# Scores and mask on 64-row tiles, roots seeded by the exponential, norm's scale on ACT, new orders on all engines

## The reference, cut to what matters

```python
qkv = x @ Wqkv                        # 3 x 1024
q, k, v = heads of 64 channels, 16 heads
q = l2norm(q) * qs ;  k = l2norm(k) * ksc
q = q * cos * scale + rotate_half(q) * sin * scale
k = k * cos * inv   + rotate_half(k) * sin * inv
# windows of 32 queries, each sees its own and the former window's 64 keys
sim = einsum('bhwie,bhwje->bhwij', bq, bk2) * 8.0
sim = where(mask, -max, sim)
out = einsum('bhwij,bhwje->bhwie', softmax(sim, -1), bv2)
x = x + out @ Wo
xn = (x - mu) / sqrt(var + 1e-5) * g + bln
a, gate = split(xn @ W1 + b1)
x = x + a * gelu(gate) @ W2 + b2
```

## Time and profile before

| | before |
|---|---|
| median of three runs | 1,781.34 us (1,781.17 to 1,782.97) |
| profiled execution, its own time | 1,780.26 us |
| span of that execution in the profile | 1,778.4 us |
| mean granted TensorE clock, share of full | 0.986 |
| PE, DVE busy | 1,708.9, 1,512.6 us |
| ACT, POOL busy | 1,350.4, 1,355.7 us |
| DMA queue of SP | 261 MB, 57.8% of 16 engines' span |

### The profile page before, as it was taken

How to read it: one execution, slowest core, us unless ns; L and a number is a source line. 1 busy time by engine, 2 the same in 40 slices (tenths; PEclk the granted TensorE clock), 3 DMA queues, 4 the chain that set the end, 5 groups by cost and what they waited for, 6 DMA issues and landing times.

```text
span 1778.4 us, 53112 instructions
## 1 busy us (share of the span) xinstructions
PE 1708.9 (96%) x20416; PEld 1355.0 (76%) x20416; DVE 1512.6 (85%) x2297; ACT 1350.4 (76%) x2689; POOL 1355.7 (76%) x2035
## 2 busy tenths in 40 slices
PE   7999968999999999999999999999999999999986
PEld 5666646888888888788888788887888888888864
DVE  5666648999999999999999999999899999999973
ACT  6777846787777777787777788787777887777763
POOL 6767658878788787778878787878878787887850
PEclk9999989999999999999999999999999999999996
DMA  3567706465865646765566656558464666656462
GB/s 115 184 234 262 254 10 159 107 148 120 223 141 132 145 107 139 213 143 139 123 147 191 152 123 146 124 127 236 112 161 104 149 177 168 147 117 146 109 152 63
DMA packets 101340, 264.54 MB, mean 149 GB/s; under 512 B 26720, under 2 KB 34912, under 8 KB 101088
## 3 DMA queue, kind: packets, MB, share of 16 engines
q1 hardware_dynamic: 101088, 261.13, 57.8%
HBM read 45.02 MB, written 27.26 MB: 41 GB/s over the span
## 4 chain that ended last, share of the span: by engine, by line
PE 81%; issue 2%; DVE 1%; ACT 1%; POOL 1%; POOLq 0%; ACTq 0%; DVEq 0%
PE ps L1462 12%; PE ps L1497 10%; PE ps L1479 10%; PE ps L1464 10%; PE ps L1463 10%; PE ps L1518 9%; PE ps L1568 7%; PE ps L1507 5%; PE ps L1579 3%; PE ps L1492 2%; PE ps L1537 1%; PE ps L1545 1%; DVE rot L1136 1%; PE ps L1554 1%; PE ps L1529 1%
## 5 line engine op out<-in xcount | busy, mean ns | idle before, releaser
L1136 DVE TENSOR_TENSOR rot<-ps,rope_l 128x1024 f32<-128x1024 f32 x384 | 461.8, 1213 | 100.9 <-ACT sq L1283 84.8
L1031 POOL TENSOR_TENSOR rot<-rot 128x512 f32<-128x512 f32 x384 | 485.8, 1288 | 31.5 <-DVE rot L1136 31.5
L1293 ACT ACTIVATE un<-ps 128x512 f32<-128x512 f32 x384 | 224.6, 598 | 237.9 <-PE ps L1464 229.8
L1462 PE MATMUL ps<-w_t,xs_hi 128*128 128x512 f32 x768 | 374.9, 488 | 12.5 <-DVE rot L1136 7.6
L1072 POOL TENSOR_TENSOR rot<-rot,rnorm 128x1024 f32<-128x1024 f32 x192 | 365.5, 1904 | 21.3
L1464 PE MATMUL ps<-w_t,xs_lo 128*128 128x512 f32 x768 | 304.7, 397 | 0.0
L1463 PE MATMUL ps<-w_t,xs_hi 128*128 128x512 f32 x768 | 303.6, 395 | 0.0
L1283 ACT ACTIVATE sq<-ps 128x512 f32<-128x512 f32 x384 | 229.1, 597 | 34.6 <-PE ps L1464 20.1
L1311 ACT ACTIVATE kT<-ps 64x512 f32<-64x512 f32 x384 | 226.3, 589 | 23.7 <-PE ps L1479 20.3
L1479 PE MATMUL ps<-ident_s,rot 128*128 128x128 f32 x1536 | 234.8, 275 | 8.6 <-ACT kT L1311 3.4
L1112 DVE TENSOR_REDUCE ssum<-sq 128x16 f32<-128x1024 f32 x192 | 232.5, 1211 | 9.8 <-ACT sq L1283 9.8
(11 more groups left out here) (121 smaller groups left out, 3093.2 us busy)
## 6 DMA issues: line engine op xcount, KB each, us to landing
vk<-un SPq DMA_DIRECT2D x1440, 128.0 KB, 2.3
w_t<-weights_dram SPq DMA_DIRECT2D x48, 512.0 KB, 6.9
weights_dram<-u_split SPq DMA_DIRECT2D x12, 1024.0 KB, 5.1
weights_dram<-qk_split SPq DMA_DIRECT2D x24, 512.0 KB, 4.0
raw<-wqk_dram SPq DMA_DIRECT2D x24, 256.0 KB, 4.9
wvt_s<-wvt_dram SPq DMA_DIRECT2D x12, 256.0 KB, 4.3
wo_s<-wo_dram SPq DMA_DIRECT2D x12, 256.0 KB, 4.7
w_s<-w_dram SPq DMA_DIRECT2D x6, 341.0 KB, 3.8
```

What stands on the lines that cost most here:

```text
L1031: last = G.tensor_tensor(cos[:, :, s, :], cos[:, :, s, :], sin[:, :, 1 - s, :], ALU.add)
L1136: V.tensor_tensor(dst, src[:, None, :, :].broadcast_to([P, 2, H // 2, D]), tab[:, :, None, :].broadcast_to([P, 2, H // 2, D]), ALU.mult).t ...
L1462: M.matmul(bank, x_hi, w_t[:, j, 0, :], start=True, stop=False)
```

## The change

- **kT** loses its zeros and its second copy: [128, pairs, keys] with the first head of a pair in rows 0 to 63 and the second in rows 64 to 127. ACT copies all 128 rows at once (four copies a unit in place of eight). The memset clears only the 32 columns ahead of the first window.
- **Scores**: each matmul contracts 64 rows of one head with 64 columns; 64 of them a tile in place of 32. The head of a pair picks the row half of the array and the PSUM bank, the window picks 32 columns. The mask is eight matmuls of 64 rows by 32 columns, each with 512 moving columns, in place of two of 64 by 128. The heads stand in the banks in another order, and DVE's scale of the probabilities writes them back in the old one.
- **The root**: the sums are clamped by POOL; the first guess is ACT's exponential of the sum's bits read as an integer; POOL does two Newton steps of four operations (one of them now a TENSOR_SCALAR).
- **The norm's** scale and shift go from DVE to ACT (`feed_scale`).
- **All five orders** are new, with the banks of the projections (`PJ_BANK`, `PJ_BEFORE`) and the order in which SP renews the weights; W2 is loaded ahead of the last value copies of a layer.

The core of the diff:

```diff
-        kT = sb("kT", [P, 2, PAIRS, WIN + T])
+        kT = sb("kT", [P, PAIRS, WIN + T])
...
-                    G.memset(kT[:, 0, :, :], 0.0)
-                    G.memset(kT[:, 1, :, :], 0.0)
+                    G.memset(kT[:, :, 0:WIN], 0.0)
...
+                    pool.wait_ge(ss_d.sem, ss_d.at(n, 2 * t + 1))
+                    G.tensor_scalar(ssum[:, t, :], ssum[:, t, :], 1e-24, None, ALU.max).then_inc(cl_g.sem, 1)
...
-                    pool.wait_ge(seed_d.sem, seed_d.at(n, t))
+                    pool.wait_ge(seed_a.sem, seed_a.at(n, t))
                     y, s = rnorm[:, t, :], ssum[:, t, :]
-                    for i in range(3):
-                        at = 12 * t + 4 * i
+                    for i, c in enumerate(ROOT_STEPS):
+                        at = 8 * t + 4 * i
...
-                        G.tensor_tensor(newton[:, :], thrice[:, i, :], newton[:, :], ALU.subtract).then_inc(newton_g.sem, 1)
+                        G.tensor_scalar(newton[:, :], newton[:, :], -0.5 * c, 1.5 * c, ALU.mult, ALU.add).then_inc(newton_g.sem, 1)
...
-                    V.tensor_scalar(ssum[:, t, :], ssum[:, t, :], 1e-24, None, ALU.max).then_inc(cl_d.sem, 1)
-                    dve.wait_ge(cl_d.sem, cl_d.at(n, t))
-                    V.tensor_scalar(rnorm[:, t, :].bitcast(I32), ssum[:, t, :].bitcast(I32), -0.5, RSQRT_SEED,
-                                    ALU.mult, ALU.add).then_inc(seed_d.sem, 1)
...
-                    V.tensor_tensor(prob[:, t, :].rearrange("p (h k) -> p h k", h=H), tile_scores(t),
-                                    linv[:, t, :, None].broadcast_to([P, H, 2 * WIN]), ALU.mult).then_inc(pn_d.sem, 1)
+                    pairs = prob[:, t, :].rearrange("p (a hp k) -> p hp a k", hp=2, a=PAIRS)
+                    inv = linv[:, t, :].rearrange("p (hp a) -> p hp a", hp=2)[:, :, :, None].broadcast_to([P, 2, PAIRS, 2 * WIN])
+                    V.tensor_tensor(pairs, tile_scores(t).rearrange("p (hp a) k -> p hp a k", hp=2), inv, ALU.mult).then_inc(pn_d.sem, 1)
...
-                    V.tensor_scalar(xg[:, :], xg[:, :], cur[:, u[1] % 2, 0:1], cur[:, u[1] % 2, 1:2], ALU.mult, ALU.add).then_inc(xh_d.sem, 1)
...
-                        for hp in range(2):
-                            rows = slice(64 * hp, 64 * hp + 64)
-                            last = S.activation(kT[rows, hp, pairs, WIN + t * P:WIN + (t + 1) * P], src[rows], ACT.Copy)
+                        last = S.activation(kT[:, pairs, WIN + t * P:WIN + (t + 1) * P], src, ACT.Copy)
...
+                    act.wait_ge(cl_g.sem, cl_g.at(n, t))
+                    S.activation(rnorm[:, t, :], ssum[:, t, :].bitcast(I32), ACT.Exp, bias=root_shift[:, 0:1], scale=ROOT_SLOPE).then_inc(seed_a.sem, 1)
...
+                    S.activation(xg[:, :], xg[:, :], ACT.Identity, scale=col[:, 0:1], bias=col[:, 1:2]).then_inc(xh_a.sem, 1)
...
-                    for hp in range(2):
-                        rows = slice(64 * hp, 64 * hp + 64)
-                        M.matmul(ps[:, SO[t] + hp, :], wpick[rows, t, :], wmask[rows, :, :].rearrange("p a k -> p (a k)"), start=True, stop=False)
+                    for k in range(4):
+                        for hp in range(2):
+                            rows = slice(64 * hp, 64 * hp + 64)
+                            M.matmul(ps[32 * k:32 * k + 32, SO[t] + hp, :], wpick[rows, t, 32 * k:32 * k + 32], wmask[rows, :, :].rearrange("p a k -> p (a k)"),
+                                     start=True, stop=False)
                     for a in range(PAIRS):
                         for k in range(4):
                             w = 4 * t + k
-                            out_s = ps[32 * k:32 * k + 32, SO[t] + a // 4, (a % 4) * P:(a % 4 + 1) * P]
-                            last = M.matmul(out_s, qT[:, par, a, 32 * w:32 * w + 32], kT[:, :, a, 32 * w:32 * w + 64],
-                                            start=False, stop=a % 4 == 3)
+                            for hp in range(2):
+                                rows = slice(64 * hp, 64 * hp + 64)
+                                out_s = ps[32 * k:32 * k + 32, SO[t] + hp, a * 2 * WIN:(a + 1) * 2 * WIN]
+                                last = M.matmul(out_s, qT[rows, par, a, 32 * w:32 * w + 32], kT[rows, a, 32 * w:32 * w + 64],
+                                                start=False, stop=a == PAIRS - 1)
```

More of the change, by code:

```diff
@@ L18 @@
+import math
 from contextlib import ExitStack
@@ L1075, in step @@
                     after, u, last = ((m, s + k) for k in (1, 0, -2))
[L1076 to L1079 removed]
                     feed_rstd(last)
+                    turn(u, 1, 0)
+                    clamp(u, 1)
                     shift_lo(after)
[L1082 removed]
                     norms(u, 1)
@@ L1087, in step @@
                     turn(after, 0, 0)
+                    clamp(after, 0)
+                    norms(after, 0)
+                    normalise(after, 0, 0)
+                    turn(after, 0, 1)
+                    normalise(after, 0, 1)
                 pipeline(pool, step)
@@ L1226, in step @@
                 def step(m, s):
-                    after, u, before, last = ((m, s + k) for k in (1, 0, -1, -2))
+                    after, u, before, last, oldest = ((m, s + k) for k in (1, 0, -1, -2, -3))
+                    rope(u, 0, 1, 0)
+                    rope(u, 0, 1, 1)
+                    soft_sum(before, 0)
+                    feed_4(oldest)
+                    soft_top(before, 1)
+                    feed_1(last)
+                    soft_shift(before, 1)
+                    feed_2(last)
+                    soft_scale(before, 0)
+                    rope(u, 1, 0, 0)
+                    feed_3(last)
+                    rope(u, 1, 0, 1)
+                    sums(u, 1, 0)
+                    feed_norm(last)
+                    sums(u, 1, 1)
+                    rope(u, 1, 1, 0)
                     rope(u, 1, 1, 1)
-                    soft_scale(before, 1)
+                    soft_sum(before, 1)
                     feed_hidden(last, 0)
                     soft_top(u, 0)
+                    soft_scale(before, 1)
                     soft_shift(u, 0)
```

156 lines of the change are left out of this document (70 added, 86 removed).

## The result

| | before | after |
|---|---|---|
| median of four runs | 1,781.69 us | 1,753.76 us (1,745.96 to 1,755.60) |
| ratio to before, 95% interval | | 0.984 (0.981 to 0.986) |
| span of the profiled execution | 1,778.4 us | 1,752.2 us |
| median and mean of the 45 full units | 30.89, 30.95 us | 29.81, 30.39 us |

The kernel became faster by 28 us, where 78 were forecast. A unit's length is read from the starts of POOL's product that writes `rtok`, which comes once a unit. The last row says already that there are two parts to explain: the typical unit became 1.1 us shorter, not 1.7, and some units are much longer than the typical one, which was hardly so before.

A forecast was written before the change was run, and what follows sets the result against it. PE was taken to bound the loop: 2.1 us a unit saved, 1.7 kept after DVE's waits, times 46 units is 78 us, so 1,780.3 becomes 1,702 and the median 1,703. Range 1,680 to 1,730, chance 0.57; 1,680 to 1,790, 0.79.

The forecast's parts named there:

- The bound: Long loop: PE sets the pace at 30.87 us a unit, with DVE's own work at 29.1 us.
- The array as the old stage's limit: Old scores stage: streaming columns, not issue, makes each group of four matmuls take 0.11 us.
- two row groups beside each other: New scores: 64-row matmuls on both row groups run at once, each further pair costing 0.11 us, not 0.22.
- the load not the limit: New scores: small matmuls aren't held by load latency; four loads of 128 columns follow by 0.11 us, here 32.
- rival (b): Scores rounds don't shrink because the load made their 0.11 us; PE saves 0.1 us a unit, 1,772 to 1,790; chance 0.08.
- Sixteen rounds at 56 ns, 0.90 us: New scores stage: each round of 8 records takes about 56 ns, so 16 rounds take 0.90 us.
- rival (c): Scores stage of 136 pairs held by PE's instruction supply; slower, 1,854 us at 22 ns a pair, 1,947 at 29.5; chance 0.16.
- The 25 ns of the page "TensorE: Matmul & The Clock Gate" of the Trainium skill: Matmul starts never under about 25 ns apart: 136 starts 3.4 us a tile, kernel some 110 us slower; not adopted.
- The mask: Mask ahead of the scores: eight matmuls beside each other take 0.27 us, where two took 0.32.
- The stage: Mask and scores together: 1.17 us in place of 2.21, saving 1.04 a tile, 2.1 us a unit.
- The 0.4 us a unit for the new orders: Unit taken as 29.2 us, not PE's 28.8, since the orders are new and DVE has waits.
- rival (a): New orders lose the gain through late ropes or copies holding PE; unit 29.8 to 30.8 us, 1,730 to 1,777; chance 0.14.

The follow-up runs named there:

- half: The changed kernel with head pairs 4 to 7 left out of the scores stage, so 64 of its 128 pairs of instructions are gone; 1,663.5 us.
- newscores: The kernel before with only the new scores, mask, key layout, key copies and softmax scale; 1,767.1 us, 0.993 of before.
- cols32: The changed kernel with each scores product taking 32 of its 64 key columns, same number of instructions; 1,750.2 us.
- padded: The whole changed kernel with 243 one-column matmuls added in nine places ahead of values stages; 1,745.9 us, 0.982 of before.
- paced: The changed kernel with the old two-matmul mask and 181 one-column matmuls added in the projections of four units; 1,745.2 us, 0.978 of before.

## Why the prediction was wrong, point by point

- **The bound.** Right. PE bounds the loop before and after, and half shows that it would go on to do so down to 28.3 us.
- **The array as the old stage's limit; two row groups beside each other; the load not the limit.** Right: sixteen records go in two rounds of 56 ns, and rival (b) falls.
- **Sixteen rounds at 56 ns, 0.90 us.** This is the step that failed. It took the pace of a burst's first pairs for that of 128 pairs. Two rounds go at 56 ns, the third at 75, the rest at 67 to 123, and the products take 1.35 us. The text named the doubt itself, in rival (c): the first pairs "may have been queued while PE drained". The pace fits that. The bound was set at 29.5 ns a pair, the rival priced at 22, and the truth, 1.35 us for 128, is 10.5 ns. With the mask it is 1.72 us for 136, 12.6 ns: under break-even at 16.3, so the sign held and the gain shrank. It would have been better to give values between 7 and 16 ns a chance of their own.
- **The 25 ns of the page "TensorE: Matmul & The Clock Gate" of the Trainium skill** (section "Wait — 56ns, not 53.3ns?"). They gave an estimated 3.4 us a tile; 1.72 was measured. Over eight tiles the rule doesn't hold.
- **The mask.** 0.27 forecast; 0.23 us from its first matmul to the first product, 0.34 in the chain with the pieces cut otherwise. Its eight matmuls are worth 0.1 us a stage against the old two, in the change.
- **The stage.** 1.17 forecast, 1.72 measured: a saving of 0.48 a tile and 0.96 a unit, not 2.1. 30.89 - 0.96 = 29.93; 29.81 was measured. 46 such units are 50 us, not 78.
- **The 0.4 us a unit for the new orders.** Not needed: PE hardly waits for another engine, and half's unit follows PE. With the orders and roots of before (newscores) the kernel is 13 us slower, 5 us of it in the typical unit.
- **Nothing foreseen at the borders.** No step of the sum had stops of PE for its own instructions. The mean unit is 0.58 us above the median one, 0.06 before: 0.52 times 45 units is 23 us. PE's list of waits, 300 to 1,700 us, sums to 23.2 us, 19.3 of them called issue, and to 2.7 before; what the lowered clock costs behind a stop comes on top. 50 - 23 = 27, and 28 was measured.
- **The range.** It held the result, by way of rival (a) (1,730 to 1,777), whose mechanism was not at work. Rival (c), priced only as a loss, was the right mechanism at a milder rate.
- **ACT, DVE, POOL.** These groups are the after of the earlier trace rows:

```profile
L1300 ACT ACTIVATE kT<-ps 128x512 f32<-128x512 f32 x192 | 113.5, 591 | 3.9 <-PE ps L1486 0.6
L1334 ACT ACTIVATE rnorm<-ssum,root_shift 128x32 f32<-128x32 int32 x96 | 29.9, 311 | 3.3 <-POOL ssum L1040 3.3
L1372 ACT ACTIVATE xg<-xg,cur 128x256 f32<-128x256 f32 x48 | 28.5, 594 | 3.3 <-DVE xg L1200 3.3
L1170 DVE TENSOR_TENSOR prob<-ps,linv 128x1024 f32<-128x1024 f32 x96 | 116.8, 1217 | 0.0
L1057 POOL TENSOR_SCALAR newton<-newton 128x32 f32<-128x32 f32 x192 | 41.6, 217 | 16.8
L1040 POOL TENSOR_SCALAR ssum<-ssum 128x32 f32<-128x32 f32 x96 | 27.6, 288 | 44.4 <-DVE ssum L1117 44.4
```

The key copies (591 ns), POOL's small steps (217 and 288 against 300) and the softmax scale, unchanged at 1,217 ns, came as forecast. The seed took 311 ns, not 220, and the norm's scale 594, not 418: these two ACT forms, one with integers in and one with a scale and a bias for each partition, are dearer here than the plain square that I had taken as their measure. None of this reached the end of a unit.

**What stays open.** Why PE goes on only 0.9 to 1.7 us after a packet has landed isn't known. That heavy data traffic is what makes a packet begin late is read from the two happening together; no run changed the traffic and left the blocks as they were. That 24 pairs are stored up is read from the pace, not from a record of a queue. The 11 ns of a pair late in a stage were not taken apart further: cols32 leaves out columns, but no run has fewer or smaller instructions for the same number of loads and matmuls.

## What to carry to other kernels

When a change trades large instructions for small ones, divide the stage's time by its instructions and ask for the longest run of that pace in the trace; the start of a burst shows what was stored up, and not the supply. Then look at the instruction queue as at any other: bytes in packets, how many instructions a packet holds, how short the time becomes in which PE runs through one, and when the next packet has landed. Under about 4.5 us a block here PE began to stop, most of all beside heavy data traffic, and two kernels with the same loop differed by 4% by where the packets ended in it. A part of a change is to be judged with the order that it was made for: the orders and roots of this one cost 2.6% with the old key layout, and with the new they were worth 5 us in the typical unit, while 8 us more hung on where the borders fell.

## What the runs showed of the hardware that I had not expected

- PE's pairs of small load and matmul on eight tiles: 7 ns a pair for the first sixteen, 9.5 to 15 from the 24th on, and 13 late in a run of 128. On one tile 24 to 26 ns (padded), on four in turn twelve in 74 ns (paced).
- Every one of the 157 stops of over 0.45 us inside a scores stage, in thirteen runs, came at an instruction whose number is 193 modulo 256. A block run through in under 3.2 us was followed by a stop in 125 of 168 cases, over 4.5 us in 28 of 2,367. All 231 stops in that count ended 0.9 to 1.7 us after a packet of 256 instructions had landed.
- Behind a stop of 3.3 us the granted clock fell to 0.59 for 2 us, and it cost half as much again.
- A wait that is already met isn't free on PE: 51 ns in its record, 106 ns from one to the next. Two between 512-column matmuls were hidden (0.23 us from start to start), three made it 0.36 us, five 0.55; 216 of them lengthened the unit by 10 us.
- The first 512-column matmul behind small tiles costs 0.43 us, 0.2 more than its neighbours. Each switch counts.
